# A LoRA-routed feed-forward layer in split float32: sums of y in PSUM and in weight slots, a narrower plain part in two-half matmuls, the first weight chunk in two loads

## The reference

```python
w = weight[adapter_ids]
y = jnp.einsum('bsi,boi->bso', x, w)                  # stage 1
base_out = jnp.einsum('btd,od->bto', y, base_W) + base_b
logits = jnp.einsum('btd,nd->btn', y, router_W) + router_b
probs = softmax(logits);  topk_p, topk_i = top_k(probs, 8)
w = jnp.einsum('btk,btke->bte', topk_p, onehot(expert_map[topk_i]))
h = jnp.einsum('btd,erd->bter', y, A)
lora = jnp.einsum('bter,eor->bto', h * w[..., None], B) * 2.0
return x + base_out + lora
```

## Time and profile before

| what | value |
|---|---|
| median of 3 runs | 408.11 us (406.92 to 408.36) |
| the profiled execution | 407.73 us, its span 405.9 us |
| PE busy, in the span | 398.8 us (98%) |
| PE weight loads (PEld) | 371.6 us (92%) |
| DVE busy | 295.8 us (73%) |
| ACT busy | 154.9 us (38%) |
| HBM traffic | 64.6 MB, 159 GB/s over the span |
| granted TensorE clock | 1.00 of full |

### The profile page before, as it was taken

How to read it: one execution, slowest core, us unless ns; L and a number is a source line. 1 busy time by engine, 2 the same in 40 slices (tenths; PEclk the granted TensorE clock), 3 DMA queues, 4 the chain that set the end, 5 groups by cost and what they waited for, 6 DMA issues and landing times.

```text
span 405.9 us, 6358 instructions
## 1 busy us (share of the span) xinstructions
PE 398.8 (98%) x2278; PEld 371.6 (92%) x2278; DVE 295.8 (73%) x575; ACT 154.9 (38%) x236; POOL 2.0 (0%) x10
## 2 busy tenths in 40 slices
PE   7999999899999999999999999999999999999997
PEld 7889998789988999889998899989998899988996
DVE  2778985999959973788638885499754997467743
ACT  3675425563046220562216630165203643045200
POOL 0000000000000000000000000000000000000000
DMA  8999016660067602585025830468105770154002
GB/s 299 399 400 393 20 42 216 256 214 0 2 242 278 204 0 96 174 297 157 0 111 199 303 110 0 157 218 291 57 7 200 245 272 0 52 200 164 1 2 103
DMA packets 24878, 64.73 MB, mean 159 GB/s; under 512 B 2466, under 2 KB 11042, under 8 KB 24866
## 3 DMA queue, kind: packets, MB, share of 16 engines
q1 hardware_dynamic: 24290, 62.48, 42.9%
q10 hardware_dynamic: 288, 1.05, 0.8%
q0 software_dynamic: 288, 1.05, 0.6%
HBM read 56.18 MB, written 8.39 MB: 159 GB/s over the span
## 4 chain that ended last, share of the span: by engine, by line
PE 91%; DVE 4%; DMA 2%; ACT 1%; issue 1%; SPq 0%
PE y_ps L783 26%; PE y_ps L785 13%; PE pl_ps L807 6%; PE pl_ps L809 6%; PE pl_ps L808 6%; PE x_ps L821 5%; PE x_ps L820 5%; PE x_ps L819 5%; PE z_ps L819 3%; PE z_ps L820 3%; PE z_ps L821 3%; DMA w_raw<-in_wT 2%; PE y_ps L796 2%; PE w_ps L819 1%; PE w_ps L821 1%; PE w_ps L820 1%
## 5 line engine op out<-in xcount | busy, mean ns | idle before, releaser
L783 PE MATMUL y_ps<-x_split,w_hi 128*128 128x512 f32 x496 | 172.9, 394 | 1.2 <-DVE y_sum L503 1.2
L785 PE MATMUL y_ps<-x_split,w_lo 128*128 128x256 f32 x496 | 137.6, 277 | 0.0
L783 PEld LDWEIGHTS y_ps<-x_split,w_hi 128*128 128x128 f32 x496 | 93.0, 187 | 22.9 <-DVE w_lo L485 0.9
L785 PEld LDWEIGHTS y_ps<-x_split,w_lo 128*128 128x128 f32 x496 | 93.2, 188 | 0.0
L485 DVE TENSOR_TENSOR w_lo<-w_raw,w_hi 128x1024 fp32r<-128x1024 f32 x58 | 70.8, 1224 | 12.6 <-ACT w_hi L362 10.3
L354 ACT COPY y_sum<-y_ps 128x256 f32<-128x256 f32 x62 | 23.1, 373 | 122.2 <-PE y_ps L785 122.2
L362 ACT CAST w_hi<-w_raw 128x1024 fp32r<-128x1024 f32 x58 | 60.7, 1050 | 10.3 <-DMA w_raw<-in_wT 10.1
L503 DVE TENSOR_TENSOR y_sum<-y_ps,y_sum 128x256 f32<-128x256 f32 x62 | 26.1, 421 | 29.8 <-ACT y_sum L354 29.5
L807 PE MATMUL pl_ps<-pl_hi,y_hi 128*128 128x432 f32 x128 | 45.7, 357 | 0.2 <-DVE y_lo L507 0.2
L809 PE MATMUL pl_ps<-pl_hi,y_lo 128*128 128x432 f32 x128 | 45.8, 358 | 0.0
L808 PE MATMUL pl_ps<-pl_lo,y_hi 128*128 128x432 f32 x128 | 45.7, 357 | 0.0
(11 more groups left out here) (140 smaller groups left out, 600.3 us busy)
## 6 DMA issues: line engine op xcount, KB each, us to landing
w_raw<-in_wT SPq DMA_DIRECT2D x60, 512.0 KB, 3.3
res<-in_x SPq DMA_DIRECT2D x16, 512.0 KB, 4.6
x_raw<-in_xT SPq DMA_DIRECT2D x14, 512.0 KB, 5.9
out<-res SPq DMA_DIRECT2D x13, 512.0 KB, 2.6
early_raw<-in_wT SPq DMA_DIRECT2D x4, 512.0 KB, 8.7
hi_raw<-in_base_t SPq DMA_DIRECT2D x4, 368.0 KB, 9.9
st_raw<-in_base_t SPq DMA_DIRECT2D x4, 368.0 KB, 10.1
pl_raw<-in_base_t SPq DMA_DIRECT2D x2, 576.0 KB, 12.1
```

Source lines behind the costliest of these rows:

```text
L783: nc.tensor.matmul(y_ps[:, c % 2, :], w_hi[:, s, k, :], x_split[:, k, :, :].rearrange("p s t -> p (s t)"), start=(k == 0), stop=False)
L785: mm = nc.tensor.matmul(y_ps[:, c % 2, 0:T], w_lo[:, s, k, :], x_split[:, k, 0, :], start=False, stop=(k == KC - 1))
```

## The change

- NP goes from 288 to 112, so a half of the other outputs is NH = 456 wide and the plain part PL is 256 wide. Hi and lo of the plain weight lie side by side: y_hi meets both in one matmul 512 wide, y_lo meets hi in one 256 wide. The two halves of the sum are joined after (`ar_part` on ACT, a DVE add before the logits, two DVE adds in `add_plain`).
- The wider blocks need room in SBUF. The three block sums are written by DVE to three PSUM banks (`s_ps`, the banks of z, w and v). Their hi and lo parts, split once per element, lie in weight slots 2 and 3. So SP loads the next element's chunks 2 and 3 only once the w bank is done, and at place c ACT and DVE prepare chunk c+2.
- In elements 2 to 7 the bias adds come one at place 6 and one after the last chunk, and the fourth sum moves behind the gates.
- Element 0: the first weight chunk comes in two loads, two small loads go to ACT's queue, the base weight comes upper half first and is split block by block, and two products are added into `res` halfway (`p1_done`, `p1_added`).

The diff, cut to its core:

```diff
-    NP = 288
+    NP = 112
+        s_hi = sb("s_hi", [P, 3, KH, P], F32R, over=at_w + 2 * 4 * KC * P)
+        s_lo = sb("s_lo", [P, 3, KH, P], F32R, over=at_w + (W_SLOTS + 2) * 4 * KC * P)
...
+        s_ps = bank("s_ps", [P, 3, 512])
+        z_ps, w_ps, v_ps = (s_ps[:, i, :] for i in range(3))
...
-                    if c + W_SLOTS < OC or not last:
+                    if c + W_SLOTS < OC or (not last and c < W_SLOTS + 2):
                         sp.wait_ge(y_ps_done, OC * b + c + 1)
                         load_w(this if c + W_SLOTS < OC else nxt, (c + W_SLOTS) % OC)
...
                     load_x(b + 1)
+                    sp.wait_ge(w_ps_done, b + 1)
+                    for c in (2, 3):
+                        load_w(nxt, c)
...
+            for j in range(PIECES):
+                k = slice(j * KP, (j + 1) * KP)
+                sp.dma_start(w_raw[:, 0, k, :], wT[bass.ds(id0, 1), 0, :, k, :].rearrange("a p k o -> (a p) k o")).then_inc(w0_in[j], 16)
...
-                    if not last or c + 3 < OC:
-                        adapter_hi(b, c + 3)
+                    if not last or c + 2 < OC:
+                        adapter_hi(b, c + 2)
...
-                    if not last or c + 3 < OC:
-                        adapter_lo(b, c + 3)
+                    if not last or c + 2 < OC:
+                        adapter_lo(b, c + 2)
...
+            block_lo(1, B00, r00)
+            block_sum_1()
+            block_lo(2, B10, r10)
             routing_logits(0)
+            t1_lo()
+            for t in range(NT):
+                dve.wait_ge(res_in[t], 16)
+                dve.wait_ge(p1_done, t + 1)
+                add(t, N2, (w_ps, x_ps)[t][:, 0:NH]).then_inc(p1_added, 1)
+            block_lo(3, B11, r11)
             routing_gates(0)
...
+                for t, part in ((1, 0), (0, 0), (1, 1), (0, 1)):
+                    for k in PLAIN_ORDER[:KC - 2] if part == 0 else PLAIN_ORDER[KC - 2:]:
...
+                        nc.tensor.matmul(pl_ps[:, t, 0:2 * PL], hi, pl_split[:, k, :, :].rearrange("p s n -> p (s n)"), start=(k == 0), stop=False)
+                        mm = nc.tensor.matmul(pl_ps[:, t, 0:PL], lo, pl_split[:, k, 0, :], start=False, stop=(k == KC - 1))
...
+                product(w_ps, y_block(0, 0), B00).then_inc(p1_done, 1)
+                product(x_ps, y_block(0, 1), B00).then_inc(p1_done, 1)
+                pe.wait_ge(blocks_lo_done, 2)
+                pe.wait_ge(p1_added, 1)
+                product(w_ps, y_block(1, 0), B10, begins=False)
```

More of the change, by code:

```diff
@@ L157, in adaln_ffn_kernel @@
         pl_in = [sem(f"pl_in{h}") for h in range(2)]
-        st_in = [sem(f"st_in{j}") for j in range(KH)]
+        upper_in = sem("upper_in")
+        lower_in = sem("lower_in")
         b_in = sem("b_in")
@@ L201, in adaln_ffn_kernel @@
         ar_done = sem("ar_done")
+        ar_part_done = sem("ar_part_done")
+        ar_sum_done = sem("ar_sum_done")
+        p1_done = sem("p1_done")
+        p1_added = sem("p1_added")
         shifted = sem("shifted")
@@ L401, in plain_hi, with block_hi @@
                 nc.scalar.copy(pl_hi[:, k, AR:PL], pl_raw[:, k, AR:PL]).then_inc(pl_hi_done, 1)
[L403 to L411, removed]
+            def block_hi(block_of, src):
+                nc.scalar.copy(st_hi[:, :, block_of, :], src).then_inc(blocks_hi_done, 1)
             def element(b, last=False):
@@ L417, in element @@
                         make_y_hi(b, c // 2)
-                    if not last or c + 3 < OC:
-                        adapter_hi(b, c + 3)
[L420 to L429, removed]
+                    if not last or c + 2 < OC:
+                        adapter_hi(b, c + 2)
+                    if isinstance(b, int) and b == 1 and c == 2:
+                        act.wait_ge(t_done, 3)
+                        nc.scalar.copy(st_hi[:, :, T4, :], st_raw[:, :, T4, :]).then_inc(t4_hi_done, 1)
+                    if isinstance(b, int) and b == 1 and c == 6:
+                        act.wait_ge(t_done, 4)
+                        nc.scalar.copy(st_hi[:, :, T3, :], st_raw[:, :, T3, :]).then_inc(t3_hi_done, 1)
+                sums_hi(b)
+                ar_part(b)
                 exponential(b)
@@ L583, in make_hwt_lo, with add_bias @@
                                         ALU.subtract).then_inc(hwt_lo_done, 1)
-            def add_bias(b):
-                for t in range(NT):
-                    dve.wait_ge(res_in[t], 16 * (b + 1))
-                    nc.vector.tensor_tensor(res[:, t, :], res[:, t, :], bias[:, :], ALU.add).then_inc(res_biased, 1)
+            def add_bias(b, t):
+                dve.wait_ge(res_in[t], 16 * (b + 1))
+                nc.vector.tensor_tensor(res[:, t, :], res[:, t, :], bias[:, :], ALU.add).then_inc(res_biased, 1)
             def add(t, cols, ps):
@@ L609, in stage2 @@
                 add(1, N2, z_ps[:, 0:NH]).then_inc(z_added, 1)
+                if second:
+                    t3_lo()
+                else:
+                    fourth(b)
                 dve.wait_ge(x_ps_done, x_adds(b, 2))
@@ L614, in stage2 @@
                     fourth(b)
-                    fourth_lo(b)
-                if not last:
+                fourth_lo(b)
+                if not last and not second:
                     make_x_lo(b + 1)
@@ L828, in s_block @@
             def s_block(i):
-                return [(lambda j, s=s: s[:, j, i, :]) for s in (s_hi, s_lo)]
+                return [(lambda j, s=s: s[:, i, j, :]) for s in (s_hi, s_lo)]
             def lora_b(t, dst, cols, begins=False):
```

301 lines of the change are left out of this document (157 added, 144 removed).

## The result

The changed kernel takes 439.51 us (median of 4 runs, 438.35 to 442.54), the kernel before 407.93 on the same chip: ratio 1.079 (95% interval 1.073 to 1.085), +31.6 us. The forecast was +24.0. The sign and the main place of the loss (stage 1) were as forecast, but the sum was a quarter short. The profiled execution took 442.54, with a span of 440.7, and is the slowest of the four; the other three took 438.35, 438.87 and 440.15.

A forecast was written before the change was run, and what follows sets the result against it. PE was taken as the bound, busy throughout at full clock from element 2 on. Start -0.8, element 0 +4.3, element 1 +3.2 and -1.3, elements 2 to 7 +18.5, end +0.1 gave +24.0: 432 us, range 424 to 440.

The forecast's parts named there:

- The chain that decides: Stage 1 of elements 2 to 7: w_lo made two chunks ahead comes late, +3.50 us per element.
- The clock falls in the gaps: Rival: PE's clock drops to 1.2 GHz in stage 1 of seven elements, +18.7 us each, 563 us; chance 0.02.
- The cost of a restart: Behind each wait for w_lo, PE needs 0.05 us to see the semaphore.
- the start: Kernel start: half of the first weight chunk lands sooner, shortening PE's 0.97 us wait; -0.8 us.
- PE costs columns: All elements: PE time follows matmul columns; 1056 fewer in each of elements 1 to 7, -0.42 us per element.
- The odd chain: Stage 1, behind odd chunks: copy through w_lo to PE's start takes 3.94 us against 2.77, a 1.17 us wait.
- PSUM sums: Three block sums written to PSUM: taken as 0 extra; rival has them dear, up to 4.9 us more, 437; chance 0.10.
- Stage 2 of the later elements: Elements 2 to 7, stage 2: PE waits for nothing; the narrowest cover is 1.5 us.
- Element 0's stage 2: Element 0: PE waits 3.3 us at `p1_added` and 1.0 us for hwt_lo; +4.3 us.
- Element 1's stage 1: Element 1: waits of 2.42, 1.18 and 1.33 us before chunks 3, 5 and 7; 27.2 us against 24.0, +3.2.
- No stage 1 stalls: Rival: the chain from copy to w_lo's end takes 2.5 us, so stage 1 never waits; 406.1 us, chance 0.03.
- Late weights: Rival: chunk 2's late-issued load lands 3.9 us late in 7 elements, +27 us, 459 us; chance 0.03.

The follow-up runs named there:

- Early adds: Changed kernel with DVE's two adds of half-done products into `res` moved ahead of the logits in element 0: 437.41 us, ratio 1.0736.
- late adds: Changed kernel with DVE's two adds of half-done products into `res` one split later, behind block B11's, in element 0: 442.78 us, ratio 1.0879.
- three ahead kernel: Changed kernel with ACT and DVE preparing chunk c+3 again instead of c+2, so splits are three ahead from chunk 4 on: 417.38 us, ratio 1.0254.
- old start: Early adds kernel with chunk 0's weight in one load, small loads back on SP's queue, masks made later: 435.48 us, ratio 1.0665.
- one load with early small loads: Early adds kernel with chunk 0's weight in one load, small loads left on ACT's queue: 441.93 us, ratio 1.0809.
- halves with late small loads: Early adds kernel with small loads back on SP's queue, chunk 0's weight still in two loads: 436.40 us, ratio 1.0694.
- mended kernel: Changed kernel with splits three ahead, early adds, small loads on SP's queue, transposes inside z, block sum 4 and T2's split moved: 409.75 us, ratio 1.0043.

## Why the prediction was right or wrong, point by point

The chain that decides was right, and the experiments show it. Where the sum failed is that it priced every wait by its own length. Two steps were wrong. The clock: the rival "The clock falls in the gaps" got 0.02 and nothing in the sum, and in the profiled execution stretches at half clock behind two of the waits cost 4.5 us (3.0 in element 0, 1.5 in element 1). The cost of a restart, taken as 0.05 us, was 0.1 us more for each of the 21 waits, 2.1 us in all. A third term had the wrong sign: the start, forecast -0.8 us, came out at +1.2 in the profiles, since the small loads moved to ACT's queue stood in it at nothing. The points in turn:

**PE costs columns.** Right. Stage 2 fell as said: the distance from the copy of chunk 7 to the next chunk 0 went from 29.21 to 28.90 us, -0.3 where -0.42 was forecast. The 224 and 112 wide matmuls, bounded between 0.30 and 0.53 us for all four, start at 276.79, 276.90, 276.96 and 277.12 in the trace, about 0.4 us in all.

**The odd chain.** Right in every link up to w_lo. Chunk 3 in the changed kernel, ACT, then DVE, then PE:

```profile
240.73 0.37 ACT L376 COPY y_sum<-y_ps 128x256 f32<-128x256 f32 x1 [2.61 <-PE y_ps L832]
241.59 0.62 ACT L380 CAST y_hi<-y_sum 128x512 fp32r<-128x512 f32 x1 [0.49 <-DVE y_sum L526]
242.12 1.05 ACT L384 CAST w_hi<-w_raw 128x1024 fp32r<-128x1024 f32 x1
```

```profile
242.00 0.29 DVE L540 TENSOR_TENSOR s_ps<-s_ps,y_sum 128x128 f32<-128x128 f32 x1
242.42 0.69 DVE L530 TENSOR_TENSOR y_lo<-y_sum,y_hi 128x512 fp32r<-128x512 f32 x1
243.20 1.22 DVE L508 TENSOR_TENSOR w_lo<-w_raw,w_hi 128x1024 fp32r<-128x1024 f32 x1
```

```profile
244.48 0.50 PE L830 MATMUL y_ps<-x_split,w_hi 128*128 128x512 f32 x1 [1.01 <-DVE w_lo L508]
244.81 0.28 PE L832 MATMUL y_ps<-x_split,w_lo 128*128 128x256 f32 x1
244.93 0.40 PE L830 MATMUL y_ps<-x_split,w_hi 128*128 128x512 f32 x1
```

From the copy to w_lo's end it is 244.42 - 240.73 = 3.69 us, to the hundredth the value of the earlier trace rows. What was mis-sized is the restart behind it, "PE needs 0.05 us to see the semaphore". PE does start 0.06 us later, but its first matmul gives way after 0.33 us and not 0.23: 0.1 us more for each wait. The stage was 23.37 us from copy to copy where the forecast gives 22.9: 0.3 us is the restart at three waits, and the rest is chunks that took 2.82 instead of 2.77 us (chunk 1 in every element from 2 on, and some of those behind a wait), which is the open pace of the last section. Per element it was +3.7 instead of +3.1, on six elements 3.9 us. Of these 1.8 are the restart, some 1.3 the slower chunks and what element 2 has over the others, and 0.8 the smaller gain in stage 2.

**PSUM sums.** The value taken, zero, holds. The sums take 0.29 to 0.30 us, 0.01 more than in SBUF, and start 0.2 us apart in both kernels. The step of 65 ns between SBUF and PSUM that the Trainium skill gives in Perfetto Trace Analysis (Optimizing Scalar/DVE Operations) does not show in these durations, and y_lo stays ahead of the cast's end. The rival fell.

**Stage 2 of the later elements.** Right: PE waited nowhere in it.

**Element 0's stage 2.** The wait at `p1_added` was 3.0 us (forecast 3.3) and the one for hwt_lo 1.0 (1.0). But the stretch grew by 7.4 and not 4.3 us. The step that failed is the rival "The clock falls in the gaps", given 0.02, argued from the 1.20 us of gaps of the earlier trace rows, which are two waits of 0.7 us at most. This kernel has far longer ones. The rival as written, all of stage 1 at half clock and 563 us, did not happen either: the clock fell for about 3 and 7 us (from the granted clock of the windows here and below). Windows of the changed kernel over the wait and behind it:

```profile
42.00:44.00 2.00, 0.98 (x5) 0.55 (x3) 1.90 (x11) 2.00 (x3) 0.00 (x0) 1.00 0.46 145
44.00:45.00 1.00, 0.00 (x0) 0.00 (x0) 1.00 (x1) 1.00 (x2) 0.00 (x0) 1.00 0.02 8
45.00:46.00 1.00, 0.03 (x1) 0.06 (x1) 1.00 (x3) 1.00 (x2) 0.00 (x0) 0.65 0.00 0
46.00:47.00 1.00, 1.00 (x3) 0.90 (x4) 1.00 (x2) 0.27 (x1) 0.00 (x0) 0.50 0.07 16
...
51.00:52.00 1.00, 1.00 (x4) 0.85 (x3) 1.00 (x2) 0.00 (x0) 0.00 (x0) 0.50 0.00 0
52.00:53.00 1.00, 1.00 (x7) 0.89 (x6) 1.00 (x2) 0.00 (x0) 0.00 (x0) 0.94 0.00 0
```

Granted 0.50 is 1.2 GHz. The 456-wide matmuls behind the wait start 0.38 us apart instead of 0.21:

```profile
45.97 0.72 PE L864 MATMUL s_ps<-st_hi,y_hi 128*128 128x456 f32 x1 [2.99 <-DVE res L617]
46.49 0.58 PE L865 MATMUL s_ps<-st_lo,y_hi 128*128 128x456 f32 x1
46.87 0.58 PE L866 MATMUL s_ps<-st_hi,y_lo 128*128 128x456 f32 x1
```

The next 16 matmuls, from 45.97 to 52.17 us, take 2.9 us more than 16 at full clock, and then the clock is back. Early adds took this fall away (one profile), and behind the longer wait of late adds all four means are below 1, so that the wait opens the fall is shown; how often one of 3 us does is not (in the three ahead kernel's profile 2.9 us didn't). It happened in the profiled run but not in the two fastest (mean clock 1.000, 438.35 and 438.87).

**Element 1's stage 1.** The longest wait was 2.1 us (forecast 2.42), but +5.0 was measured and not +3.2, and again the clock is in it:

```profile
77.00:81.00 4.00, 2.08 (x7) 1.78 (x8) 3.83 (x5) 3.44 (x4) 0.00 (x0) 0.80 0.40 136
81.00:85.00 4.00, 4.00 (x20) 3.45 (x19) 2.29 (x5) 0.93 (x3) 0.00 (x0) 0.77 0.09 13
```

The copies of chunks 2 and 3 are 6.06 us apart, where the late adds profile, with the same wait and full clock, has 4.54. That is 1.5 of the 1.8 us missing; the restart at three waits is the other 0.3.

**The start.** The sign was wrong: +1.2, not -0.8. The term priced the two halves and left the small loads moved to ACT's queue at nothing, without naming what hid them. With them early, PE starts about 1 us later and the weight of chunk 2 lands later. The halves bring the first matmul forward but not the copy of chunk 2, since DVE's copy of y, behind w_lo, then sets when chunk 2 may start; the term looked at PE's first weight alone. Part of the +1.2 is chance: the profile of the kernel before, at 17.44, is the earliest of three with its start (the other two 18.24 and 18.28), so 0.3 to 1.2 us is what the profiles bear out.

**The other rivals.** "No stage 1 stalls" fell with the 21 waits. "Late weights" fell too: no cast in an element after the first waited long for a load, and PE never waited for one after its first chunk.

Summed, for the profiled execution: 2.0 (start) + 3.9 (elements 2 to 7: restart, slower chunks, stage 2) + 3.1 and 1.8 (elements 0 and 1: clock 4.5, restart 0.3 and 0.1 more) + 0.1 is, but for rounding, the 10.8 us between 34.8 and 24.0. Without a fall of the clock an execution was at 438.4, still 6.4 us above the 432 forecast; that part is the start, the restart and the slower chunks.

## What to carry to other kernels

How far ahead an operand is prepared is a budget of time: before taking one stage off it, add up the longest chain between the event that starts the preparation and its end, from the trace, and hold it against what is left. Here 3.7 us had 5.5, and then 2.8, and one number cost 26 us, while the 1% of columns (1056 of some 107000 per element) that it made room for were worth 2. When a change opens waits of 2 to 5 us on a TensorE that never idled, add what comes behind them: the restart, and stretches at half clock, in some executions and not in others. A tiny load issued ahead of the first large ones has to be priced like any other. And a start time read from one profile may be off by a microsecond: compare a later mark, in several profiles.

## What the runs showed of the hardware

- Behind a wait of about 1 us, PE's first 512-wide matmul gave way after 0.33 us instead of 0.23, at a granted clock of 1.00.
- After a wait of 5.0 us (late adds) the granted clock fell in the profile, and the mean clock was below 1 in all four runs. After 3.0 us it was at 0.50 for 6 us in the changed kernel's profile and at 1.00 after 2.9 us in the three ahead kernel's. After the 2.1 us in element 1 four profiles show a fall (changed, early adds, old start, one load with early small loads) and two don't (late adds, halves with late small loads). The profile of one load with early small loads also has 0.61 between 60 and 64 us, behind a wait of 1.8 us for hwt_lo; early adds have that wait too, and 1.00 there.
- PE's start moved between 7.41 and 8.72 us in five profiles of the same start code.
- Writing 128 columns to PSUM from DVE took 0.01 us longer than to SBUF.
- Some stage 1 chunks took 2.83 us and others 2.77, both at a granted clock of 1.00, while the wide products of stage 2 kept their pace (456 columns in 0.206 to 0.208 us). Both paces were seen within one execution: elements 3 to 6 of the mended kernel had 2.77 from chunk 3 on, element 7 had 2.83, and the changed kernel mixes them. The cause was not tried.
